# More room for the descriptors of GpSimd's DMAs, and the second half's expert ranking moved into the first three seats: an attention and mixture-of-experts layer on one core

## What is computed

```python
x = L0_attn_x                                   # (1, 2048, 256)
x = x + layernorm(attention(layernorm(x)))      # 16 heads, weights as codes * scales
def ffn(x, Wr, Wg, Wu, Wd):                     # E = 8 experts, K = 2 of them for each row
    probs = softmax(x @ Wr)
    topk_w, topk_idx = top_k(probs, 2)
    topk_w = topk_w / sum(topk_w)
    combine = sum_k(topk_w[k] * onehot(topk_idx[k]))
    h = silu(einsum('bsh,ehi->besi', x, Wg)) * einsum('bsh,ehi->besi', x, Wu)
    y = einsum('besi,eih->besh', h, Wd)
    return einsum('bse,besh->bsh', combine, y)
x = x + layernorm(ffn(layernorm(x)))
```

## Time and profile before

| | us |
|---|---|
| median of 3 runs | 2086.07 |
| the profiled execution | 2085.8 |
| its span (first to last instruction) | 2084.1 |
| TensorE busy | 1971.1 |
| VectorE busy | 1750.8 |
| GpSimd busy | 1528.5 |
| ScalarE busy | 1418.9 |

### The profile page before, as it was taken

How to read it: one execution, slowest core, us unless ns; L and a number is a source line. 1 busy time by engine, 2 the same in 40 slices (tenths; PEclk the granted TensorE clock), 3 DMA queues, 4 the chain that set the end, 5 groups by cost and what they waited for, 6 DMA issues and landing times.

```text
span 2084.1 us, 33186 instructions
## 1 busy us (share of the span) xinstructions
PE 1971.1 (95%) x10902; PEld 1703.5 (82%) x10902; DVE 1750.8 (84%) x2706; ACT 1418.9 (68%) x2686; POOL 1528.5 (73%) x1317
## 2 busy tenths in 40 slices
PE   7999999999999999999999999999999999976882
PEld 5888888888888888888888888888888888865772
DVE  6889889998989888988999898988898888975344
ACT  4777767776777767776777677776777677763444
POOL 2679778887779777977888777977797787974222
PEclk9999999999999999999999999999999999987886
DMA  4667767786678667775777666766677576832343
GB/s 98 159 156 185 177 142 177 172 192 150 165 163 190 158 151 163 179 162 136 163 165 175 147 152 156 179 151 144 155 177 167 135 165 147 210 92 92 115 127 104
DMA packets 173040, 322.66 MB, mean 155 GB/s; under 512 B 47686, under 2 KB 105798, under 8 KB 172870
## 3 DMA queue, kind: packets, MB, share of 16 engines
q1 hardware_dynamic: 169798, 312.15, 64.0%
q0 software_dynamic: 3072, 8.39, 1.3%
HBM read 35.68 MB, written 18.35 MB: 26 GB/s over the span
## 4 chain that ended last, share of the span: by engine, by line
PE 82%; SPq 4%; POOL 3%; ACT 3%; DVE 3%; issue 2%; DMA 1%; another core or an unknown queue 1%; POOLq 0%; ACTq 0%
PE ps_a L750 20%; PE ps_s L622 14%; PE ps_s L624 13%; PE ps_s L623 13%; PE ps_a L751 10%; PE ps_a L622 3%; SPq L396 3%; PE ps_a L624 3%; PE ps_a L623 3%; POOL pT_both L519 2%; ACT probs L1038 1%; DVE part_max L1394 1%; POOL x_rows L595 1%; PE ps_s L928 1%
## 5 line engine op out<-in xcount | busy, mean ns | idle before, releaser
L519 POOL TENSOR_TENSOR pT_both<-pT,pT_both 128x512 fp32r<-128x512 f32 x1016 | 1291.2, 1301 | 339.9 <-ACT pT_both L1055 337.8
L1038 ACT ACTIVATE probs<-ps_s,shift 128x1024 f32<-128x1024 f32 x512 | 566.6, 1110 | 275.6 <-DVE shift L1403 275.5
L750 PE MATMUL ps_a<-pT_both,v_both 128*128 128x512 f32 x2048 | 744.3, 397 | 0.7 <-POOL pT_both L519 0.5
L1055 ACT ACTIVATE pT_both<-pT 128x512 fp32r<-128x512 f32 x1016 | 606.7, 629 | 162.8 <-DMA pT<-probs 128.8
L1419 DVE STREAM_TRANSPOSE probs<-probs 128x1024 f32<-128x1024 f32 x508 | 614.5, 1229 | 56.8 <-ACT probs L1038 55.9
L1394 DVE TENSOR_REDUCE part_max<-ps_s 128x1 f32<-128x1024 f32 x512 | 612.5, 1215 | 20.6 <-PE ps_s L624 19.0
L751 PE MATMUL ps_a<-pT_both,v_both 128*128 128x256 f32 x2048 | 573.9, 280 | 0.0
L750 PEld LDWEIGHTS ps_a<-pT_both,v_both 128*128 128x128 f32 x2048 | 385.5, 188 | 86.1 <-POOL pT_both L519 1.3
L622 PE MATMUL ps_s<-kT_hi,qT_hi 128*128 128x512 f32 x1024 | 406.6, 397 | 11.7 <-ACT probs L1038 8.6
L623 PE MATMUL ps_s<-kT_lo,qT_hi 128*128 128x512 f32 x1024 | 403.3, 394 | 0.0
L624 PE MATMUL ps_s<-kT_hi,qT_lo 128*128 128x512 f32 x1024 | 401.9, 392 | 0.0
(11 more groups left out here) (202 smaller groups left out, 2596.6 us busy)
## 6 DMA issues: line engine op xcount, KB each, us to landing
pT<-probs SPq DMA_DIRECT2D x2032, 128.0 KB, 2.3
x_rows<-zeros SPq DMA_DIRECT2D x46, 128.0 KB, 2.1
xg<-x_rows SPq DMA_DIRECT2D x46, 128.0 KB
y_rows<-y_sb SPq DMA_DIRECT2D x46, 128.0 KB
pT<-in_L_attn_x SPq DMA_DIRECT2D x4, 512.0 KB, 5.6
codes<-in_L_attn_wk_codes SPq DMA_DIRECT2D x16, 128.0 KB, 2.4
scales<-in_L_attn_wk_scales SPq DMA_DIRECT2D x64, 32.0 KB, 2.9
codes<-in_L_attn_wo_codes SPq DMA_DIRECT2D x16, 128.0 KB, 2.3
```

The source lines that it names most:

```text
L519: pool.tensor_tensor(pT_lo[:, p, :].rearrange("p (i n) -> p i n", i=Q4), pT[:, s % 2, :, g, t:t + 2, :].rearrange("p i t q -> p i (t q)"), ...
L750: nc.tensor.matmul(out_both, v_hi[:, h % 2, k, :], move, start=k == 0, stop=False)
L1038: nc.scalar.activation(out, src, ACT.Exp, bias=shift[:, s % SLOTS, r:r + 1], scale=SCALE, accum_out=sums[:, s % SLOTS, r, g:g + 1])\
L1055: nc.scalar.activation(pT_hi[:, p, :].rearrange("p (i n) -> p i n", i=Q4), pT[:, s % 2, :, g, t:t + 2, :].rearrange("p i t q -> p i (t q)" ...
```

## The change

1. `dynamic_dma_scratch_size` goes from 1024 to 4096 bytes of each partition.
2. To have the room, the one-column tiles `zero` and `warm` go; `zero` becomes the first column of `zeros`, and `warm` a column of `wr_raw`. `zeros` (128x256) is therefore filled at the very start of GpSimd's program, in the place of `zero` (128x1), and not after the first weights.
3. On VectorE, `beaten(1)`, `tie_broken(1)` and `choose(1)` go from ahead of `seat_lo(0)` into slots 0, 1 and 2.
4. All that follows from the ranking of part 1 moves three slots later on VectorE; on TensorE `count_all(1)` goes from slot 0 to 3, `count_places(1)` from 3 to 6, and the first `expert_of` of part 1 from slot 10 to 12. `weights_of(0)` and `weights_of(1)` also move three slots.

```diff
-        zero = sb("zero", [P, 1], f32)
...
-        warm = sb("warm", [P, 1], f32)
...
         zeros = sb("zeros", [P, D], f32)
+        zero = zeros[:, 0:1]
         wr_raw = sb("wr_raw", [P, DC, E], f32)
+        warm = wr_raw[:, 0, 0:1]
...
-            pool.memset(zero[:, :], 0.0).then_inc(sm["ident_set"], 1)
+            pool.memset(zeros[:, :], 0.0).then_inc(sm["zeros_set"], 1)
             pool.memset(ident[:, :], 0.0).then_inc(sm["ident_set"], 1)
-            pool.wait_ge(sm["ident_set"], 2)
+            pool.wait_ge(sm["ident_set"], 1)
...
-            pool.memset(zeros[:, :], 0.0).then_inc(sm["zeros_set"], 1)
...
-                if n >= 10:
-                    expert_of(SEATS[0] + n - 10)
-                if n == 0:
+                if n >= 12:
+                    expert_of(SEATS[0] + n - 12)
+                if n == 3:
                     count_all(1)
-                if n == 3:
+                if n == 6:
                     count_places(1)
...
-            beaten(1)
-            tie_broken(1)
-            choose(1)
             seat_lo(0)
             for n in range(NS + 4):
                 hidden_lo(n - 2)
                 seat_lo(n + 1)
                 hidden(n)
+                if n == 0:
+                    beaten(1)
                 if n == 1:
+                    tie_broken(1)
+                if n == 2:
+                    choose(1)
+                if n == 4:
                     seat_starts(1)
-                if n == 2:
+                if n == 5:
                     seat_rows()
-                if n == 4:
+                if n == 7:
                     take_places(1)
-                if n == 5:
+                if n == 8:
                     rows_of(1)
-                if n == 6:
+                if n == 9:
                     seat_experts(1)
...
-    nc = bacc.Bacc("TRN2", target_bir_lowering=False, num_devices=1, dynamic_dma_scratch_size=1024)
+    nc = bacc.Bacc("TRN2", target_bir_lowering=False, num_devices=1, dynamic_dma_scratch_size=4096)
```

More of the change, by code:

```diff
@@ L1189, in _ @@
                 if n == LAST:
-                    nc.scalar.activation(warm[:, :], zero[:, :], ACT.Sqrt).then_inc(sm["warm_done"], 1)
+                    nc.scalar.activation(warm, zero[:, :], ACT.Sqrt).then_inc(sm["warm_done"], 1)
                 probs_hi(n - 1, 0)
@@ L1874, in _ @@
                 hidden(n)
+                if n == 0:
+                    beaten(1)
                 if n == 1:
+                    tie_broken(1)
+                if n == 2:
+                    choose(1)
+                if n == 4:
                     seat_starts(1)
-                if n == 2:
+                if n == 5:
                     seat_rows()
-                if n == 4:
+                if n == 7:
                     take_places(1)
-                if n == 5:
+                if n == 8:
                     rows_of(1)
-                if n == 6:
+                if n == 9:
                     seat_experts(1)
-                if n == 9:
+                if n == 12:
                     weights_of(0)
-                if n == 12:
+                if n == 15:
                     weights_of(1)
```

## The result

| | before | changed |
|---|---|---|
| median, us (20 runs each) | 2083.91 | 2089.55 |
| lowest to highest, us | 2079.54 to 2089.61 | 2086.84 to 2094.41 |
| the profiled execution, us | 2085.8 | 2089.05 |
| its span, us | 2084.1 | 2087.3 |

The ratio of the runs is 1.0024, with a 95% interval of 1.0017 to 1.0032. The changed kernel is slower by 5.6 us of median; the 0.2% that I had set as the least that can be told lie inside the interval. The forecast of 2086.4 was "no difference"; the range of 2081.0 to 2092.0 holds the time. The kernel before had 3 runs when the forecast was made, with a median of 2086.07; its 20 runs give 2083.91.

What follows compares the result with a forecast made beforehand. The prediction took TensorE, busy 95% of the span and nearly all in attention, as the bound. Its terms, -0.7 + 0.3 + 0.7 = +0.3 us on 2085.8 and a 0.3 offset to the median, gave 2086.4 us, range 2081.0 to 2092.0.

Steps and rivals of the forecast that it cites:

- (a): GpSimd's sends of part 0: more room removes both holes, so seat 0's rows arrive 3.5 us sooner, or 0.
- (c): Ranking of part 1 on VectorE, moved into slots 0 to 2: costs +0.3 us, bounds 0 and 3.9.
- (b): First seat on TensorE: register loads leave 1.5 us of the earlier arrival, counted as -0.7 us because of half clock.
- (d): Seats beside part 1's sends: sends without holes lose 13.8 us instead of 13.1, +0.7, ends -5.4 and +8.2.
- the rival of the sooner clock: First seat: TensorE's clock rises sooner, so -3.1 us there and -2.1 in sum, 2084.0 us; chance 0.08.
- the breath: Part 1's sends: holes let TensorE recover; without them the loss goes to 21.3 us, 2093.9 us in all; chance 0.21.
- a loss over 18 us: Sign of being wrong: such a loss beside part 1's sends makes (d) the failed step.
- the rival of the cheaper burst: Part 1's sends: one burst costs less than bursts with holes, -5.8 us in sum, 2080.3 us; chance 0.16.
- (e): The rest, such as filling `zeros` first, fetches and `weights_of`: 0 us.
- `turn_x(0)` at 1903.8 right behind the last `expert_of`: Sign of being right: seat 0's first transpose waits for TensorE's register loads, not for the load of xg.
- a transpose before 1903.5: Sign of being wrong: seat 0 transposed that early would mean the register loads moved, which was thought impossible.

Runs made afterwards that it cites:

- e2: The changed kernel with the descriptor room left at 1024 bytes, so only the order moves: 2084.76 us, ratio 0.9990 to the kernel before.
- e1: The kernel before with 4096 bytes for descriptors, ranking and slots as before: 2095.77 us, ratio 1.0036 to the kernel before.
- e10: The changed kernel itself, run again in another job: 2059.76 us, ratio 0.9980 to the kernel before.
- e11: The changed kernel with part 1's sends and part 0's fetches spread over slots, and TensorE's 12 register loads moved into slots: 2058.35 us, ratio 0.9973.
- e12: The same kernel as e9, run again in another job: 2086.03 us, ratio 1.0004 to the kernel before.
- e9: The changed kernel with GpSimd pausing by four small fillings ahead of each part's eighth and fifteenth send: 2058.78 us, ratio 0.9977.

## Why the prediction was right or wrong

The time lies 3.2 us from the forecast and inside the range, and in part that is luck. What was forecast is a change of +0.3 us, and the change is +5.6. The sum was built on the median of 3 runs, 2086.07; against the 2083.91 of 20 runs it would have given 2084.2, so 2.2 us of the miss don't show in the number. Of the mechanism, (a) and (c) hold, (b) came out with the wrong sign and (d) too small.

**(a) The holes: right.** It is room; all four holes are gone, and the last send of part 0 starts 19.8 us after the first instead of 23.4. e2, with 1024 bytes and the new order, has them still (23.3 us from first to last), and e1, with 4096 and the old order, lacks them (19.8 us). Seven sends to 1024 bytes is the estimate that came of the 9 write descriptors for each DMA engine of the Trainium skill ("DMA: Bandwidth & Descriptors", The descriptor swizzle), and the sends agree. The fetches don't, 16 in a row without a hole with the same 1024 bytes; why is open.

**(b) The first seat: the failed step.** I wrote that the register loads "follow from the router's products, not from the sends, and the change does not move them". The first half is true and the second doesn't follow: the router's products are made beside the sends, and their words are held up like any other. The term came out as +1.4 us of first seat in place of -1.5, which stood in the sum as -0.7 (+3.6 in e1). That the loads are what bounds the first seat is right: in e10, where nothing is held up, it comes at 27.4 right behind them, 1.1 us sooner than in the kernel before, and in e11, with the loads out of the way, at 24.2. In e12 it comes at 26.8, just behind the last load's check of 1901.1, though its row names the load of `xg`. The clock moved with the transpose: 0.50 for the 6.5 us after it and 0.99 behind, as before, so the rival of the sooner clock had nothing for it.

**(c) The ranking: right.** Forecast +0.3. Nine slots, from the first transpose of seat 0 to that of seat 9, take 21.3 us before, 21.8 changed, 21.9 in e2 and 21.3 in e10. VectorE has 4.53 of 4.90 us busy in the window at 1909.40, and even so little is lost.

**(d) The sends of part 1: right in kind, too small.** Forecast a loss of 13.8 us, measured 18.0, so +4.9 in place of +0.7. By the rate of the fetches alone, 0.75 for each us, it would have been 15.1. I mixed in the sends' own rate, 0.56, which is that of sends with holes: the very thing that the change removes. My argument against the breath, that a TensorE that stands still sends fewer words and the loss saturates, holds only as far as its price goes: the rival had 21.3, a price per send, and 18.0 is between. A single word held for 11 us was not in any of my cases. The sign that I had named for (d) as the failed step, a loss over 18 us, is missed by a hair (17.95). One reading in the rival of the cheaper burst is wrong too: a mean clock of 0.70 over 23.0 us is 13.8 us at half clock, which cost 6.9 us of work at full clock, and not 6.9 us at half clock.

**(e) and the sum.** Nothing was seen in the rest. In the profile: +1.4 + 4.9 + 0.5 + 0.7 (the fetches) = +7.5 against 7.0 measured from the first send on; the medians differ by 5.6. The way it went is the rival of the breath, which I gave 0.21 and 2093.9; its price for the sends was 3.3 us too high, and it lacked the router's share.

The profiled execution of the changed kernel also shows a trap in my list of signs. "`turn_x(0)` at 1903.8 right behind the last `expert_of`" looks met, even early, at 1902.85, and a transpose before 1903.5 stood there as a sign of being wrong. It is that early only because this execution reached its first send 3.8 us sooner, by the scatter of the attention.

## What to carry to other kernels

Before a pause in a DMA queue is removed, look at which waits of other engines end inside it: here both long waits of ScalarE beside part 1's sends (3.95 and 3.69 us) ended 0.1 us into a hole, and that could have been read before the change. Indirect DMAs of GpSimd are cheaper beside TensorE's work in small groups than in one row, and a plain DMA, where the addresses allow it, cost nothing. Compare stages from a common event and not by absolute times, when the stage ahead scatters by more than the effect, and measure on more than one occasion: the change costs 0.24% on one and gains 0.20% on another.

## What the runs showed of the hardware

- Beside an unbroken row of indirect DMAs of GpSimd (one each 1.27 us), words of TensorE to ScalarE arrive up to 11 us late, and SyncE gets the same word as late as ScalarE. The granted clock falls with TensorE's idling, to 0.60 in that window; it is 1.00 where sends are paced or plain. 64 bytes a row in place of 1024 change nothing (17.5 and 18.0 us lost), and plain DMAs of the same engine cost 0.2. A word of ScalarE to VectorE within the same row is not late: `hid` starts at 1932.28, behind the `silu_g` of 1931.93 to 1932.25.
- In the job of e9 to e11 this was absent, and the kernel before took 2063.16 us instead of 2083 to 2086. It was there in four other jobs, one of them on the chip with the same number. Whether it hangs on the chip or on what else runs at the time is open. So is through which part of the chip the words and the indirect DMAs meet: no run here shows it.
- A register load on TensorE's queue (load, register instruction and check) takes 0.65 us of the queue, and 12 of them ahead of the first seat are 7.7 us (1895.1 to 1902.8); with them spread over the slots, and both pacings, e11 took 2058.35 us beside the 2059.76 of e10, which can't be told apart.
